# Small-head attention of a gated block stack: the order of scores, shifts, exponentials and additions on three engines

## The chip, the cores and the metric

The kernel runs on one core of a Trainium2 chip. The time is the device time of one execution in microseconds, and a lower one is better. The engines of the core are TensorE (PE; its weight loads are listed apart, as PEld), VectorE (DVE), ScalarE (ACT), GpSimd (POOL) and SyncE (SP, which here only issues DMAs). Each works off its own queue in the order written and waits on semaphores that the others raise.

## The reference, cut to what matters

The program takes `x` of 64 batch entries, each 128 rows of 128 values, and adds eight gated layers to it, four of them cross-attention to a context of 77 rows of 64 values for each batch entry. The change touches layer 0 and layer 2 of these, attention with 16 heads of 8 dimensions, which share one function:

```
x = x + tanh(g) * ATT(layernorm(x), ctx)
ATT: q = x @ Wq (+bq), k = ctx @ Wk (+bk), v = ctx @ Wv (+bv), each cut into 16 heads of 8
     scores = einsum('bhqd,bhkd->bhqk', q, k) / sqrt(8)
     out = einsum('bhqk,bhkd->bhqd', softmax(scores), v);  return concat(out) @ Wo (+bo)
```

All the other layers (expert feed-forward layers, two more attentions, a coupling network) stand unchanged.

## The kernel before, in words

`small_head_attention` (L535) is called twice, as stage `l0x` (L2947) and as stage `l2x` (L2951, with biases). A stage works through the 64 batch entries ("blocks" below, one block being one batch entry) in 16 rounds of `GROUP` = 4. What is done once for a round (the statistics and the normalizing of x, its transposes, queries, keys, two halves of the values) is spread over the four block slots of the round. Within a block the 16 heads are two halves, A and B, of eight heads, each half with a PSUM tile `scores[h]` of two banks.

The steps of one block, `j`, with the engine that takes each:

- `score` (TensorE, L751): six matmuls of half-precision parts write a half's scores.
- `max` (DVE, L965) reduces them to a maximum per head; `split_max` (GpSimd, L680 and L682) cuts it in two bf16 parts; `mt` (TensorE, `turn_max`, L758) transposes them; `m` (ScalarE, `fetch_max`, L882) brings them to `mT`; `shift` (TensorE, L767) adds minus the maximum to the scores in PSUM.
- `exp` (ScalarE, L889) writes the probabilities of the half to `probs`.
- The 1232 probabilities of a row are turned as ten pieces in three units: `turn0` (four pieces, needs only half A), `turn1` (four) and `turn2` (two), TensorE, L782. `high0` to `high2` (ScalarE, L895) and `rest0` to `rest2` (DVE, L969) make a high and a low half-precision part of each, and `weigh0` to `weigh2` (TensorE, L801, with filling matmuls L805) multiply by the values.
- `divide` (DVE, L977 and L981), `turn_o` (TensorE, L811), `o` (ScalarE, L901), `output` (TensorE, L815), and `add` (DVE, L989) into x.

`turned[0]` serves turn0 and turn2; `turned[1]` serves turn1, and holds the results of turn_o and output too, so turn1 waits until add of the block before has read it (`s_x`).

The order of the work is written by hand. Each engine has a text with the names of its steps in one slot; `slots` (L599) makes a list of it for the four slots of a round, and `skewed` (L43) runs this list for each round, with a lag for each step, so that steps of different rounds interleave. The last number of a step's entry, `ago`, tells of which block it is: 0 is the block `j` of the slot, 1 the block before it, 2 the one before that. In the kernel before, turn1, turn2, weigh0 to weigh2, divide, turn_o, output and add are of the block before, all else is of the block itself.

Work that belongs to the round goes in at `mid` and `end` of TensorE's text: the first slot has `q` at the end (queries, L716), the second `k` (keys, L721), the third `v0` (values of two blocks, L739), and the fourth `v1` (L739) at `mid` and `x` (transposes of the next normalized x, L362) at the end. The result of v0 and v1 is brought out by DVE (`block_values`, L957: v0 at `begin` of the fourth slot, v1 at its `mid`). All of q, k, v0, v1 and x write the same PSUM bank `pa`: `turn_x` waits on `s_vf` until block_values of v1 is done. On ScalarE, `x`, `q` and `k` are fetched at `begin` of the first three slots, and the parts of the values (L875, in two slots) or of the context (L845, in one) at `mid`.

Of the kernel before, what the change touches and what calls it, by code (L numbers as in the profile page):

```python
# [42 lines left out]
def skewed(eng, n, steps, lead):  # L43


    lead = min(lead, n)
    last = max(lag for _, lag in steps)
    assert lead % 2 == 0 and n % 2 == 0 and (n == lead or lead >= last + 2)

    def peeled(ts):  # L50
        for t in ts:
            for step, lag in steps:
                if 0 <= t - lag < n:
                    step(It(t - lag, (t - lag) // 2, (t - lag) % 2))

    peeled(range(lead))
    if n > lead:
        with eng.Fori(lead // 2, n // 2) as pair:
            for u in range(2):
                for step, lag in steps:  # L60
                    step(It(pair * 2 + (u - lag), pair + (u - lag) // 2, (u - lag) % 2))
    peeled(range(n, n + last))


def first_of(it):

    return isinstance(it.b, int) and it.b == 0
# [19 lines left out]
def nth(it, per=1, c=None, ago=0, back=0):  # L87


    value = it.b * per + ((per - 1 if c is None else c) + 1 - back - ago * per)  # L90
    return None if isinstance(value, int) and value <= 0 else value
# [110 lines left out]
class Softmax:  # L202
# [36 lines left out]
    def shift(self, dve, it, c):  # L239

        a, b = self.first[c], self.first[c + 1]
        dve.wait_ge(self.s_max, nth(it, self.nb, c))
        if (due := nth(it, self.nc_, ago=2)) is not None:
            dve.wait_ge(self.s_turn, due)
        dve.tensor_tensor(self.probs[it.par][:, a:b, :], self.view(c),  # L245
                          self.mx[it.par][:, a:b].unsqueeze(2).to_broadcast([P, b - a, self.keys]),
                          ALU.subtract).then_inc(self.s_shift, 1)

    def exponential(self, act, it, c):

        a, b = self.first[c], self.first[c + 1]
        act.wait_ge(self.s_shift, nth(it, self.nb, c))
        v = self.probs[it.par][:, a:b, :]
        act.activation(v, v, ACT.Exp, scale=self.scale).then_inc(self.s_exp, 1)  # L254
# [280 lines left out]
def small_head_attention(nc, g, name, wq, wk, wv, wo, bq=None, bk=None, bv=None, bo=None, gate=0):  # L535
# [14 lines left out]
    n = g.B // GROUP  # L550
    UNITS = [range(0, 4), range(4, 8), range(8, 10)]
    first_use = name == "l0x"
    with Stage(nc, name) as st:
# [37 lines left out]
        def half(h):  # L591

            return scores[h][:, :].rearrange("p (c f) -> p c f", f=BANK)[:, :, 0:W].rearrange("p c (h t) -> p c h t", t=KEYS)
# [5 lines left out]
        def slots(steps, order):  # L599


            out = []
            for j in range(GROUP):
                for step, lag, ago in [steps[k] for k in order[j].split()]:
                    out.append((lambda it, f=step, j=(j - ago) % GROUP: f(it, j), lag + (1 if j < ago else 0)))
            return out

        with nc.Block() as block:
# [94 lines left out]
            def _(pe):  # L703
# [5 lines left out]
                def turn_x(it):  # L709
                    if (due := nth(it, 2, ago=1)) is not None:  # L710
                        pe.wait_ge(s_vf, due)
                    fr.turn(pe, it)

                def queries(it):
                    pe.wait_ge(fr.s_xT, nth(it))
                    pe.matmul(pa[:, :], wq_s[:, :], fr.xT[it.par][:, :], start=True, stop=True).then_inc(s_q, 1)  # L716

                def keys_of(it):
                    pe.wait_ge(s_ctx[it.par], loads(it, 2))
                    pe.wait_ge(s_qlo, nth(it))  # L720
                    pe.matmul(pa[:, 0:GROUP * KEYS], wk_s[:, :], ctx2[it.par][0:CTX, :, :].rearrange("c b t -> c (b t)"),  # L721
                              start=True, stop=True).then_inc(s_k, 1)
# [32 lines left out]
                def turn_max(it, j, h):  # L755

                    pe.wait_ge(s_ml, nth(it, 8, 2 * j + h))
                    pe.matmul(scores[h][64 * h:64 * h + 64, W + 12:W + 12 + P], mh[j % 2][:, 2 * h:2 * h + 2, :].rearrange("p g r -> p (g r)"),  # L758
                              g.ident16[:, :], start=False, stop=True, skip_group_check=True).then_inc(s_mt, 1)

                def shift(it, j, h):
                    if first_of(it) and j == 0 and h == 0:
                        pe.wait_ge(g.s_made, CONSTANTS)
                    pe.wait_ge(s_mT, nth(it, 8, 2 * j + h))
                    for c in range(2):
                        rows = slice(64 * h + 32 * c, 64 * h + 32 * c + 32)
                        last = pe.matmul(scores[h][:, c * BANK:c * BANK + W], mT[j % 2][rows, :],  # L767
                                         g.minus_one[rows, :, :].rearrange("p h t -> p (h t)"), start=False, stop=True,
                                         skip_group_check=True)
                    last.then_inc(s_shift, 1)  # L770
# [42 lines left out]
                def output(it, j):  # L813
# [3 lines left out]
                steps = {"x": (lambda it, j: turn_x(it), 0, 0), "q": (lambda it, j: queries(it), 1, 0), "k": (lambda it, j: keys_of(it), 1, 0),  # L817
                         "v0": (lambda it, j: values(it, 0), 1, 0), "v1": (lambda it, j: values(it, 1), 1, 0),
                         "turn_o": (turn_o, 2, 1), "output": (output, 2, 1)}
                for h, half_name in enumerate("AB"):  # L820
                    steps["score" + half_name] = (lambda it, j, h=h: score(it, j, h), 2, 0)
                    steps["mt" + half_name] = (lambda it, j, h=h: turn_max(it, j, h), 2, 0)
                    steps["shift" + half_name] = (lambda it, j, h=h: shift(it, j, h), 2, 0)
                for u in range(3):
                    steps[f"turn{u}"] = (lambda it, j, u=u: turn(it, j, u), 2, 1 if u else 0)
                    steps[f"weigh{u}"] = (lambda it, j, u=u: weigh(it, j, u), 2, 1)
                fronts = [("", "q"), ("", "k"), ("", "v0"), ("v1", "x")]
                skewed(pe, n, slots(steps, ["scoreA turn1 turn2 weigh0 mtA weigh1 shiftA weigh2 scoreB turn0 " + mid +
                                            " turn_o mtB output shiftB " + end for mid, end in fronts]), 6)

            @block.scalar
            def _(act):
# [14 lines left out]
                def fetch_x(it):  # L847
                    fr.fetch(act, it, s_q)
# [35 lines left out]
                def exponential(it, j, h):  # L884
                    act.wait_ge(s_shift, nth(it, 8, 2 * j + h))
                    if (due := nth(it, 12, 3 * j + 2, back=6)) is not None:
                        act.wait_ge(s_turn, due)
                    dst = probs[j % 2][:, 2 * h * W:2 * (h + 1) * W].rearrange("p (c h t) -> p c h t", c=2, t=KEYS)
                    act.activation(dst, half(h), ACT.Exp, scale=scale).then_inc(s_exp, 1)  # L889
# [7 lines left out]
                def fetch_o(it, j):  # L897
                    act.wait_ge(s_oTp, nth(it, 4, j))
                    if (due := nth(it, 4, j, back=2)) is not None:
# [3 lines left out]
                steps = {"c": (lambda it, j: context_high(it), 0, 0), "x": (lambda it, j: fetch_x(it), 1, 0),  # L903
                         "q": (lambda it, j: fetch_q(it), 1, 0), "k": (lambda it, j: fetch_k(it), 1, 0),
                         "v0": (lambda it, j: fetch_v(it, 0), 2, 0), "v1": (lambda it, j: fetch_v(it, 1), 2, 0), "o": (fetch_o, 2, 1)}
                for h, half_name in enumerate("AB"):
                    steps["m" + half_name] = (lambda it, j, h=h: fetch_max(it, j, h), 2, 0)
                    steps["exp" + half_name] = (lambda it, j, h=h: exponential(it, j, h), 2, 0)
                for u in range(3):
                    steps[f"high{u}"] = (lambda it, j, u=u: high(it, j, u), 2, 1 if u else 0)  # L910
                fronts = [("x", "v0"), ("q", "v1"), ("k", ""), ("", "c")]
                skewed(act, n, slots(steps, [begin + " high1 high2 mA expA " + mid + " high0 o mB expB" for begin, mid in fronts]), 6)

            @block.vector
            def _(dve):
# [68 lines left out]
                def add(it, j):  # L984
                    x = g.x[:, bass.ts(it.b * GROUP + j, P)]
                    if biased:
# [4 lines left out]
                steps = {"stats": (lambda it, j: statistics(it), 0, 0), "norm": (lambda it, j: fr.normalize(dve, it), 0, 0),  # L991
                         "q": (lambda it, j: query_rest(it), 1, 0), "k": (lambda it, j: key_rest(it), 1, 0),
                         "v0": (lambda it, j: block_values(it, 0), 1, 0), "v1": (lambda it, j: block_values(it, 1), 1, 0),
                         "divide": (divide, 2, 1), "add": (add, 2, 1)}
                for h, half_name in enumerate("AB"):
                    steps["max" + half_name] = (lambda it, j, h=h: maximum(it, j, h), 2, 0)
                for u in range(3):
                    steps[f"rest{u}"] = (lambda it, j, u=u: rest(it, j, u), 2, 1 if u else 0)
                fronts = [("", "", "stats"), ("q", "", "norm"), ("k", "", ""), ("v0", "v1", "")]
                skewed(dve, n, slots(steps, ["maxA rest1 rest2 " + begin + " maxB divide rest0 " + mid + " add " + end  # L1000
                                             for begin, mid, end in fronts]), 6)


# [2020 lines left out]
```

## Time and profile before

| | us |
|---|---|
| median of 3 runs | 6024.17 (6015.81 to 6030.27) |
| the profiled execution | 6007.85 |
| its span | 6006.1 |
| PE busy | 5001.8 (83%) |
| PE weight loads busy | 3632.7 (60%) |
| DVE busy | 3931.2 (65%) |
| ACT busy | 2730.1 (45%) |
| POOL busy | 2168.7 (36%) |
| mean granted clock of TensorE | 0.905 |

The shares are means over the whole program. The two stages that the change touches take 604 and 593 us of the span. PE's busy time comes from instructions that overlap, so a busy PE can still be short of its peak. The granted clock is 1.00 at 2.4 GHz and 0.50 at 1.2 GHz.

### The profile page before, as it was taken

What the parts mean: (1) busy time and instruction counts of PE and PEld (TensorE: products, weight loads), DVE (VectorE), ACT (ScalarE), POOL (GpSimd) and SP (SyncE); (2) the same over time, 40 slices, a digit from 0 to 9 for tenths busy, and PEclk for the clock granted to TensorE, in tenths of its full rate; (3) what the DMA queues carried; (4) which work ended last, traced back from release to release, by engine and by line L of the source; (5) the groups of instructions that cost most, each with busy time, mean ns of one, the idle gap of its engine ahead of it and who ended that gap; (6) DMA issues with size and microseconds to landing.
All of it is one profiled execution on the core that took longest, in us unless ns stands there. A gap on an engine that the chain in (4) does not pass through costs nothing. (4 is left out here: it accounts for less than half of the span.)

```text
span 6006.1 us, 133430 instructions
## 1 busy us (share of the span) xinstructions
PE 5001.8 (83%) x41659; PEld 3632.7 (60%) x41659; DVE 3931.2 (65%) x9897; ACT 2730.1 (45%) x5454; POOL 2168.7 (36%) x3095
## 2 busy tenths in 40 slices
PE   7999898999962798069997998898898799998888
PEld 4555466888862465045555665776776577776544
DVE  4555685777766333245555776888887688887544
ACT  3444475555540233034444554555554355554344
POOL 4333100111117100644332334777775733333300
PEclk8888898999985899578888998999999899999988
DMA  1000500000011343100000000000000000000000
GB/s 37 6 4 2 242 0 14 5 5 5 5 49 43 114 136 116 47 13 6 4 3 12 1 0 9 0 0 0 0 0 5 7 2 2 2 2 6 1 11 18
DMA packets 108941, 140.24 MB, mean 23 GB/s; under 512 B 35832, under 2 KB 83256, under 8 KB 103996
## 3 DMA queue, kind: packets, MB, share of 16 engines
q1 hardware_dynamic: 100544, 120.88, 6.0%
q0 software_dynamic: 8192, 16.79, 1.0%
q8 instruction: 108, 1.77, 0.1%
q14 instruction: 97, 0.79, 0.0%
HBM read 47.44 MB, written 58.72 MB: 18 GB/s over the span
## 5 line engine op out<-in xcount | busy, mean ns | idle before, releaser
L2175 POOL TENSOR_TENSOR l3a_probs<-l3a_probs,l3a_later 128x512 f32<-128x512 f32 x256 | 320.6, 1281 | 4.9 <-DVE l3a_total L2363 4.9
L2161 POOL TENSOR_TENSOR l3a_keys<-l3a_kT,head 128x2048 f32<-128x2048 f32 x64 | 230.4, 3600 | 232.5 <-ACT l3a_kT L2288 232.5
L1590 POOL DMA_INDIRECT l1c_rows<-l_rows,l1f_slots x128 | 122.2, 955 | 456.7 <-PEq L1582 402.4
L2223 PE MATMUL l3a_scores<-l3a_keys,l3a_qT 128*128 128x512 f32 x512 | 256.5, 604 | 4.2 <-POOL l3a_keys L2161 4.2
L170 POOL TENSOR_TENSOR l1x_ve<-l1x_mv,eps 128x1 f32<-128x1 f32 x64 | 12.1, 190 | 660.6 <-DVE l1x_mv L162 660.6
L298 PE MATMUL l3a_po<-l3a_vals,l3a_probsT 128*128 128x32 f32 x2048 | 247.8, 269 | 0.1
L298 PEld LDWEIGHTS l3a_po<-l3a_vals,l3a_probsT 128*128 128x128 f32 x2048 | 246.8, 192 | 0.4 <-ACT l3a_probsT L279 0.4
L1661 POOL TENSOR_TENSOR l2f_hid<-l2f_prod,l2f_route 128x512 f32<-128x512 f32 x128 | 152.1, 1193 | 256.6 <-DVE l2f_prod L1808 253.3
L254 ACT ACTIVATE l3a_probs<-l3a_probs 128x512 f32<-128x512 f32 x256 | 161.7, 632 | 181.6 <-DVE l3a_probs L245 176.4
L965 DVE TENSOR_REDUCE l0x_mx<-l0x_scores 128x8 f32<-128x616 f32 x128 | 102.4, 800 | 192.0 <-PE l0x_scores L751 191.6
L965 DVE TENSOR_REDUCE l2x_mx<-l2x_scores 128x8 f32<-128x616 f32 x128 | 102.3, 800 | 178.7 <-PE l2x_scores L751 177.7
L1509 PE MATMUL l1e_h<-l1e_xhi,l1f_parts 128*128 128x512 f16 x640 | 204.8, 381 | 9.6 <-DVE l1e_gated L1567 8.1
L284 DVE SCALAR_TENSOR_TENSOR l1x_loT<-l1x_turned,l1x_hiT 77x512 f16<-77x512 f32 x256 | 168.7, 679 | 48.8 <-ACT l1x_hiT L277 48.7
L2161 POOL TENSOR_TENSOR l3c_keys<-l3c_kT,head 128x1232 f32<-128x1232 f32 x64 | 144.0, 2251 | 155.9 <-ACT l3c_kT L2288 155.9
L277 ACT ACTIVATE l3c_hiT<-l3c_turned 77x512 f16<-77x512 f32 x256 | 150.2, 587 | 106.7 <-PE l3c_po L298 104.1
L1102 ACT ACTIVATE l0f_relu<-l0f_h,l0f_route 128x512 f32<-128x512 f32 x256 | 157.8, 687 | 84.5 <-DVE l0f_route L1141 45.1
L2223 PE MATMUL l3c_scores<-l3c_keys,l3c_qT 128*128 128x308 f32 x512 | 191.2, 455 | 1.0 <-POOL l3c_keys L2161 1.0
L284 DVE SCALAR_TENSOR_TENSOR l3c_loT<-l3c_turned,l3c_hiT 77x512 f16<-77x512 f32 x256 | 173.8, 679 | 20.0 <-ACT l3c_hiT L277 19.9
L1567 DVE TENSOR_TENSOR l1e_gated<-l1e_h,l1e_silu 128x512 f32<-128x512 f32 x160 | 110.7, 692 | 115.1 <-ACT l1e_silu L1541 115.1
L279 ACT COPY l3a_probsT<-l3a_turned 128x512 f32<-128x512 f32 x256 | 150.3, 587 | 77.7 <-PE l3a_turned L266 77.2
L277 ACT ACTIVATE l1x_hiT<-l1x_turned 77x512 f16<-77x512 f32 x256 | 144.5, 589 | 86.1 <-PE l1x_po L298 77.0
L237 DVE TENSOR_REDUCE l3a_mx<-l3a_scores 128x4 f32<-128x512 f32 x256 | 169.8, 684 | 20.3 <-issue 16.1
(581 smaller groups left out, 17366.9 us busy)
## 6 DMA issues: line engine op xcount, KB each, us to landing
l_rows<-l0f_zeros SPq DMA_DIRECT2D x34, 1024.0 KB, 26.1
l1f_parts<-l1f_split SPq DMA_DIRECT2D x40, 512.0 KB, 3.6
l1e_x_in<-l_rows SPq DMA_DIRECT2D x40, 256.0 KB, 2.9
l1f_down<-l1f_w SPq DMA_DIRECT2D x40, 256.0 KB, 2.3
l_rows<-l1e_y_out SPq DMA_DIRECT2D x40, 256.0 KB, 2.7
l1f_w<-in_L_W SPq DMA_DIRECT2D x16, 256.0 KB, 3.3
out_x<-x_res SPq DMA_DIRECT2D x16, 256.0 KB, 2.0
x_res<-in_x SPq DMA_DIRECT2D x1, 3840.0 KB, 12.4
```

The costliest lines, as they stand in the source:

```text
L237: dve.tensor_reduce(self.mx[it.par][:, a:b], self.view(c), AX, ALU.max).then_inc(self.s_max, 1)
L254: act.activation(v, v, ACT.Exp, scale=self.scale).then_inc(self.s_exp, 1)
L277: act.activation(self.hiT[c % 2][:, :], src, ACT.Copy, scale=SPLIT_EXP).then_inc(self.s_fetch, 1)
L284: dve.scalar_tensor_tensor(self.loT[c % 2][:, :], self.ps_turn[c % 2][0:self.keys, :], SPLIT_EXP, self.hiT[c % 2][:, :], ALU.mult, ALU.sub ...
L298: last = pe.matmul(out_of(h), p[c % 2][:, cols], v, start=(i == 0), stop=(i == len(products) - 1))
L965: dve.tensor_reduce(mx[j % 2][:, 2 * h:2 * h + 2, :], half(h), AX, ALU.max).then_inc(s_max, 1)
L1102: act.activation(relu[e][:, :], ps_h[e][:, :], ACT.Relu, scale=rt.w[it.par][:, j, e:e + 1]).then_inc(s_relu, 1)
L1509: last = pe.matmul(bank[:, :], parts[p][:, w, f], x[p][:, :], start=(k == 0), stop=(k == 2))
L1661: pool.tensor_tensor(hid[k % 2][:, :].rearrange("p (e m) -> p e m", m=M), prod[k % 2][:, :].rearrange("p (e m) -> p e m", m=M), rt.w[it.pa ...
L2161: pool.tensor_tensor(keys[it.par][:, :, :, :], kT[it.par][:, :, :].unsqueeze(2).to_broadcast([P, J, G4, T]), g.head32[:, :].unsqueeze(1).u ...
L2175: pool.tensor_tensor(v, v, later[:, :].unsqueeze(1).to_broadcast([P, 4, T]), ALU.mult).then_inc(s_masked, 1)
L2223: pe.matmul(scores[c][:, 0:G4 * T], qT[it.par][:, c, :], keys[it.par][:, c, :, :].rearrange("p h t -> p (h t)"), start=True, stop=True).th ...
```

## The change

It moves steps within the hand-written orders and changes three of the `ago` numbers; no instruction is added or taken away.

- TensorE: scoreB now comes before shiftA, weigh1 and weigh2; shiftB is done one slot later (`ago` 1 for B), right behind scoreA of the next block; weigh0 comes before turn1 and turn2; turn0 stands behind the round's `mid` work, not ahead of it.
- ScalarE: expB is done one slot later, first of all; mA comes before high2; `mid` comes before expA.
- DVE: add is of two blocks before (`ago` 2) and opens the slot, behind the `end` work of the slot before rather than ahead of it; the `begin` work comes before rest1 and rest2.

```diff
@@ tensor
-                    steps["shift" + half_name] = (lambda it, j, h=h: shift(it, j, h), 2, 0)
+                    steps["shift" + half_name] = (lambda it, j, h=h: shift(it, j, h), 2, h)
...
                 fronts = [("", "q"), ("", "k"), ("", "v0"), ("v1", "x")]
-                skewed(pe, n, slots(steps, ["scoreA turn1 turn2 weigh0 mtA weigh1 shiftA weigh2 scoreB turn0 " + mid +
-                                            " turn_o mtB output shiftB " + end for mid, end in fronts]), 6)
+                skewed(pe, n, slots(steps, ["scoreA shiftB weigh0 turn1 turn2 mtA scoreB shiftA weigh1 weigh2 " + mid +
+                                            " turn0 turn_o mtB output " + end for mid, end in fronts]), 6)
@@ scalar
-                    steps["exp" + half_name] = (lambda it, j, h=h: exponential(it, j, h), 2, 0)
+                    steps["exp" + half_name] = (lambda it, j, h=h: exponential(it, j, h), 2, h)
...
                 fronts = [("x", "v0"), ("q", "v1"), ("k", ""), ("", "c")]
-                skewed(act, n, slots(steps, [begin + " high1 high2 mA expA " + mid + " high0 o mB expB" for begin, mid in fronts]), 6)
+                skewed(act, n, slots(steps, ["expB " + begin + " high1 mA high2 " + mid + " expA high0 o mB" for begin, mid in fronts]), 6)
@@ vector
-                         "divide": (divide, 2, 1), "add": (add, 2, 1)}
+                         "divide": (divide, 2, 1), "add": (add, 2, 2)}
...
                 fronts = [("", "", "stats"), ("q", "", "norm"), ("k", "", ""), ("v0", "v1", "")]
-                skewed(dve, n, slots(steps, ["maxA rest1 rest2 " + begin + " maxB divide rest0 " + mid + " add " + end
+                skewed(dve, n, slots(steps, ["add maxA " + begin + " rest1 rest2 maxB divide rest0 " + mid + " " + end
                                              for begin, mid, end in fronts]), 6)
```

## Rows read from the trace of the kernel before

**Rows 1.** busy time of each engine, granted clock (PEclk), by stretch; the two attention stages

```profile
41.00:645.00 604.00, 545.64 (x5708) 332.25 (x5707) 327.26 (x767) 280.59 (x602) 210.18 (x456) 0.84 0.02 4
...
2597.00:3190.00 593.00, 533.43 (x5694) 326.70 (x5693) 327.82 (x765) 284.28 (x602) 228.77 (x471) 0.86 0.02 4
```

**Rows 2.** the same view, two rounds of four blocks in stage l0x

```profile
229.71:264.51 34.80, 31.19 (x365) 19.70 (x365) 20.94 (x51) 17.73 (x38) 13.61 (x30) 0.95 0.03 6
...
302.06:341.85 39.79, 36.40 (x364) 21.63 (x365) 21.00 (x51) 17.73 (x38) 13.61 (x30) 0.79 0.02 4
```

**Rows 3.** instructions in time, TensorE: start us, length us, engine, line, output<-input, count, [idle before]

```profile
284.70 0.30 PE L751 MATMUL l0x_scores<-l0x_keys_hi,l0x_q_hi 32*128 32x308 f16 x2
...
285.20 0.88 PE L782 MATMUL l0x_turned<-ident,l0x_probs 128*128 128x128 f32 x6
285.91 0.17 PE L801 MATMUL l0x_po<-l0x_v_hi,l0x_p_hi 128*128 128x18 f16 x1
...
287.27 0.19 PE L801 MATMUL l0x_po<-l0x_v_hi,l0x_p_hi 128*128 128x27 f16 x1
...
288.30 0.30 PE L767 MATMUL l0x_scores<-minus_one,l0x_mT 32*128 32x308 bf16 x2
...
288.78 0.30 PE L751 MATMUL l0x_scores<-l0x_keys_hi,l0x_q_hi 32*128 32x308 f16 x2
...
289.38 0.66 PE L782 MATMUL l0x_turned<-ident,l0x_probs 128*128 128x128 f32 x4
290.73 0.33 PE L811 MATMUL l0x_turned<-ident,l0x_o 128*128 128x128 f32 x1 [0.69 <-DVE l0x_o L981]
290.99 0.24 PE L758 MATMUL l0x_scores<-ident,l0x_mh 128*64 128x128 bf16 x1
291.41 0.49 PE L815 MATMUL l0x_turned<-l0x_wo,l0x_oT 128*128 128x128 f32 x2 [0.18 <-ACT l0x_oT L901]
...
292.07 0.18 PE L739 MATMUL l0x_pa<-l0x_wv_a,l0x_ctxT 128*128 128x16 f16 x1
```

**Rows 4.** the same view, ScalarE, same block

```profile
285.89 0.87 ACT L895 ACTIVATE l0x_p_hi<-l0x_turned 128x512 f16<-128x512 f32 x2 [0.59 <-PE l0x_turned L782]
...
288.65 0.68 ACT L889 ACTIVATE l0x_probs<-l0x_scores 128x616 f32<-128x616 f32 x1 [1.18 <-PE l0x_scores L767]
290.08 0.60 ACT L895 ACTIVATE l0x_p_hi<-l0x_turned 128x512 f16<-128x512 f32 x1 [0.75 <-PE l0x_turned L782]
291.10 0.27 ACT L901 COPY l0x_oT<-l0x_turned 128x128 f32<-128x128 f32 x1 [0.42 <-PE l0x_turned L811]
291.38 0.26 ACT L882 CAST l0x_mT<-l0x_scores 64x128 bf16<-64x128 f32 x1
```

**Rows 5.** the same view, VectorE, same block

```profile
286.52 1.02 DVE L969 SCALAR_TENSOR_TENSOR l0x_p_lo<-l0x_turned,l0x_p_hi 128x512 f16<-128x512 f32 x2 [0.41 <-ACT l0x_p_hi L895]
...
289.39 0.80 DVE L965 TENSOR_REDUCE l0x_mx<-l0x_scores 128x8 f32<-128x616 f32 x1 [1.45 <-PE l0x_scores L751]
290.10 0.25 DVE L977 RECIPROCAL l0x_recip<-l0x_po 128x16 f32<-128x16 f32 x1
```

**Rows 6.** the same view, TensorE, the end of the fourth block

```profile
299.17 0.66 PE L782 MATMUL l0x_turned<-ident,l0x_probs 128*128 128x128 f32 x4
299.67 0.17 PE L739 MATMUL l0x_pa<-l0x_wv_a,l0x_ctxT 128*128 128x16 f16 x1
...
300.67 0.31 PE L811 MATMUL l0x_turned<-ident,l0x_o 128*128 128x128 f32 x1
...
302.06 0.63 PE L362 MATMUL l0x_pa<-ident,l0x_xn 128*128 128x128 f32 x4
```

**Rows 7.** the same view, VectorE, the fourth block

```profile
301.11 0.71 DVE L957 TENSOR_TENSOR l0x_v_f<-l0x_pa,piece_mask 128x240 f32<-128x240 f32 x2
```

**Rows 8.** busy time and granted clock of TensorE around a clock fall

```profile
307.00:309.50 2.50, 1.50 (x11) 1.00 0.00 0
...
310.40:313.60 3.20, 3.20 (x12) 0.50 0.00 0
```

## The prediction, made before the change was run

> **What bounds the kernel now.** Start with the stretches by stage: the two attention stages take 604 and 593 us, 1197 of the 6006 us span, and nothing else is touched, so all gain and loss lies there. TensorE is busy 90% of them, DVE 54%, ACT 47%, POOL 35 to 39% [rows 1]. TensorE bounds them, in two ways: by the short pauses in each block slot, and by its clock, granted at 0.84 and 0.86 of full. Two rounds of the same 365 matmuls (within one) take 34.80 us at a mean clock of 0.95 and 39.79 us at 0.79 [rows 2]. The time at half clock is twice the missing share: 2 x 0.05 x 34.80 = 3.5 us, and 2 x 0.21 x 39.79 = 16.7 us. So 13.2 us more at half clock cost 4.99 us: 0.38 us for each.
>
> Next the timeline of one slot at full clock, from scoreA at 284.70 [rows 3 to 5]. In offsets from scoreA: turn1 at 0.50, weigh0 1.21, weigh1 2.57, shiftA 3.60, scoreB 4.08, turn0 4.68, turn_o 6.03, mtB 6.29, output 6.71, then shiftB, and the next work at 7.37. The reader should see the pauses: before turn_o the row shows 0.69 us (for DVE's o), before output 0.18 (for ACT's oT) [rows 3]. Why turn_o is late: scoreB comes late, so maxB runs at 289.39 for 0.80, and divide is queued behind it [rows 5]. Behind such a place the clock falls: 307.0 to 309.5 has TensorE busy for 1.50 of 2.50 us at full clock, and from 310.4 on the clock is 0.50, with TensorE busy all the time [rows 8]. In the fourth slot of a round v1 covers just this pause: turn0 at 299.17, v1 at 299.67, turn_o at 300.67 and x at 302.06, with no pause noted at these [rows 6].
>
> **The change, part by part.** No instruction is added, so all rests on which wait ends last. I lay the new order out by hand with the lengths of the rows, from scoreA = 0 at full clock. The spacings between starts: score 0.50 (284.70 to 285.20), shift 0.24 (half of the 0.48 from shiftA to scoreB, which hold shift and the short weigh2; weigh2 the same), turn1 with turn2 0.71, weigh1 1.03, weigh0 1.02 (285.91 to mtA; it and weigh1 have four pieces each, so I take what 287.27 to 288.30 shows), turn0 0.50 [rows 3, 6]. A mt I take as 0.17 (an estimate, inside its length of 0.24).
>
> *A slot with no v1.* scoreA 0, shiftB 0.50, weigh0 0.74 to 1.76. ExpB starts 0.35 behind shiftB (288.30 to 288.65) and takes 0.68, ready at 1.53, so turn1 starts at 1.76 without a wait [rows 3, 4]. mtA at 2.47, scoreB at 2.64 to 3.14. maxA, at 0.70 to 1.50 (a max starts 0.6 to 0.7 behind its score, 288.78 to 289.39) and the two POOL operations (some 0.5) are done by then. high1 starts 0.69 behind turn1 (285.20 to 285.89), at 2.45, and ends at 3.05 (0.60 [rows 4]); mA is queued behind it, 0.26, so shiftA can't go before 3.39: a pause of 0.25. rest1 ends at 3.77 (the two rests take 1.02, rest1 0.69 of it), weigh1 starts at 3.83 and ends 4.86, weigh2 5.10, a pause of 0.2. ExpA (3.74 to 4.42, or to 4.93 behind a 0.59 `mid`) is ready for turn0 at 5.10. maxB now runs at 4.12 behind rest2, ends at 4.92, and is no longer in front of anything late: divide waits on weigh2's end (5.17), is done at 5.88, and turn_o starts at 5.93, a pause of 0.34 instead of 0.69. But then ACT is late: high0 starts 0.70 behind turn0, 5.80 to 6.40; o is behind it, 6.42 to 6.69 [rows 3, 4]; output goes at 6.74, a pause of 0.38 instead of 0.18. Output 0.42, next work at 7.16. So 7.16 against 7.37: **0.21 gained in each of three slots, 0.63 a round.** What stood behind output (shiftB, expB) is hidden by the next scoreA and weigh0; what that cover hides is 1.0 us. The bounds of this gain are 0 (the pauses only moved) and 0.5 (the 0.69 pause gone and output's kept at 0.18) a slot.
>
> *The fourth slot.* v1 now stands ahead of turn0. It takes 1.00 (299.67 to 300.67 [rows 6]): weigh2 ends 5.10, v1 to 6.10, turn0 at 6.10. turn_o and mtB follow without a wait, but high0 runs only at 6.80 to 7.40 and o to 7.69, so output goes at 7.74: a pause of 0.7 where v1 used to cover. Behind high0 on DVE is rest0 (to 8.12), behind that block_values of v1, 0.71 [rows 7], to some 8.8, and x on TensorE waits for exactly that. x goes at 8.83, a pause of 0.7 behind output's end at 8.16, and with its 0.6 the slot ends at 9.4. Before, from turn0 (offset 4.68, the distance in rows 3) to x took 302.06 - 299.17 = 2.89, so x was at 7.57 and the slot ended at 8.1 to 8.2. **1.3 us lost a round**; bounds 0.7 (x alone waits, the rest as before) and 1.6.
>
> *Moves at no cost.* add behind stats (1.25 us) or norm (1.1): add was already last in DVE's slot, and turn1, which needs it, is now at 1.76 instead of 0.50; if that cover went, up to 1 us in two slots. The begin work ahead of rest1 (0.47 to 0.71) lies in DVE's idle time between 1.50 and 3.05. The context copy (0.95) ahead of expA lies in the fourth slot, where v1 hides it. POOL's order is unchanged; in its fullest slot it is free about when maxB ends. SP issues two context loads a round, a round ahead, and is not moved.
>
> *Sum at full clock:* 1.3 - 0.63 = 0.67 us a round, in 2 x 16 rounds 21 us. About a third of the stages' time is at half clock (2 x 0.16 = 0.32 [rows 1]); there TensorE's parts take longer and cover most of these pauses: 21 x 0.68 = 14 us.
>
> *The clock.* By rows 2 a us at half clock costs 0.38. In three slots the longest pause falls from 0.69 to under 0.4, but the sum of the pauses changes little and they still lie close together; in the fourth slot, which had none of weight, two of 0.7 now follow each other closely. I expect to lose one place where the clock was safe and to weaken three where it fell; on balance 1 us more at half clock a round, 0.38 x 32 = 12 us. Bounds: from 7 us less (the three slots mostly stay up; the means of 0.84 become 0.94) to 5 us more (a fourth place of fall in most rounds), that is -85 to +61 us. I stay near zero, because the work per pause hardly changes.
>
> This is where the Trainium skill speaks against counting the clock at all. The trace shows a fall behind pauses of under 0.7 us each [rows 3, 8]; the page "TensorE: Matmul & The Clock Gate", section "HAM oscillation — how this bites in real kernels", ties the fall to long waits for a DMA in each tile, of which there are none here. By that page of the Trainium skill the clock term is 0 and the sum 14 to 21; by the rows it is the largest unknown.
>
> **Forecast:** 14 + 12 = 26 us slower than the profiled execution's 6007.85, that is 6034; the median of the runs shown is 16 higher, 6024.17, so 6050 us.
>
> **The rivals.**
> 1. *The clock comes back (faster).* Place: the three slots without v1, between scoreB and output. For it: the longest pause is nearly halved, and a round at 0.95 shows how much is to be had. Against: the sum of the pauses there hardly falls, and the fourth slot gets worse. Price: 4 us less at half clock a round, 0.38 x 4 x 32 = 49 gained against 14 lost: 5989. It decides from 1.2 us less a round on (0.44 / 0.38). The section "A second HAM failure mode: psum-queue depth-cycling" of the Trainium skill's page "TensorE: Matmul & The Clock Gate" tells of a clock that swings by short pauses between groups of matmuls; the falls behind the 0.69 us pauses agree with it, so the rival stays possible.
> 2. *The fourth slot is repaid.* The long slot lets DVE and ACT get ahead, and the next slots gain what it lost, or ACT is less late for output than I think: 0 to 0.1 us a round, no change, 6024 to 6028.
> 3. *A round loses its clock in the fourth slot and keeps the old falls.* 4 us more at half clock a round, 49 + 14: 6087. For it: the pauses of rows 3 still total as much. Against: TensorE at half clock has few pauses, so falls can't follow each other closely.
>
> **How the numbers follow.** The forecast's own case (6036 to 6072) 0.45, rival 1 0.23, rival 2 0.17, rival 3 0.15. A measurement of this kernel tells 0.2%, 12 us, from no change. Rival 1 gives faster 0.20 (a part of it ends within 12 us); same takes rival 2 and the edges, 0.20; slower 0.60. The range leaves out one in ten on each side: 5995 to 6095.
>
> **What would show it.** In the new profile: turn_o's wait for DVE shrinks, and output's wait for ACT's oT grows from 0.2 to 0.4 in three slots and to 0.7 in the fourth; x waits there for block_values (L957), some 0.7, where it waited for nothing; a slot with no clock fall takes 7.1 to 7.2 plus its round's work, the fourth 9.4. Wrong it would be if x waits for nothing (then v1 is not where I put it), if TensorE's clock in the two stages leaves 0.80 to 0.86, or if the other 4800 us move at all.

## The result: 3.1% faster where 0.4% slower was forecast

| | us |
|---|---|
| before, median | 6023.43 (6015.81 to 6030.27) |
| changed, median | 5839.89 (5836.92 to 5840.84) |
| ratio, 95% interval | 0.9693 [0.9681, 0.9705] |
| profiled execution | 6007.85 before, 5840.04 changed |

The forecast was 6050 in a range of 5995 to 6095: wrong in sign and outside the range.

Start again with the stretches. In each kernel I take a stage from its first query matmul to its last, 15 rounds: before first, then the changed kernel. Columns: stretch, its length, TensorE's busy time (instructions), granted clock, DMA share, GB/s.

```profile
30.30:578.30 548.00, 493.76 (x5207) 0.85 0.02 5
2585.60:3124.50 538.90, 483.12 (x5207) 0.85 0.02 5
```

```profile
30.40:500.30 469.90, 411.53 (x5206) 0.95 0.02 6
2490.30:2959.70 469.40, 408.90 (x5205) 0.94 0.02 6
```

The 15 rounds lose 78 and 70 us, 148 of the 168 us between the two spans. What lies between the stages (with the last rounds, which drain in it) goes from 2007.3 to 1990.0 us, and what follows from 2881.6 to 2878.3. So most of the change is where it was expected; its size was not.

The other 21 us are not simply a gain. No kernel here changes the instructions of those two parts, and still in the 13 traces of this case the part between takes 1975.2 to 2007.3 us and the part behind 2868.9 to 2892.1. Why is open. Where two kernels differ by 30 us or less, the lengths of the two stages tell more than the whole time, though each comes from one trace; the table below has both.

Look at the clock next. In stage l0x half-clock time falls from 2 x 0.15 x 548 = 164 us to 2 x 0.05 x 470 = 47 us, in l2x from 162 to 56. At the 0.38 us each that [rows 2] gave, that is, as an estimate, 44 and 40 us of the 78 and 70. The rest, 34 and 30 us, is a shorter round at full clock. A round of the changed kernel with no fall and one with a fall, as in [rows 2]:

```profile
167.42:198.90 31.48, 27.51 (x365) 17.87 (x365) 21.01 (x51) 16.63 (x38) 13.58 (x29) 1.00 0.03 7
231.16:264.56 33.40, 29.73 (x364) 19.09 (x365) 20.83 (x51) 16.77 (x38) 13.57 (x29) 0.90 0.02 5
```

Between these two a microsecond at half clock costs only 1.92 / 6.7 = 0.29 us; experiment e5 below gives 0.37 for the kernel before, close to the 0.38 used.

Now TensorE in the slot that answers to [rows 3], at full clock:

```profile
281.39 0.30 PE L751 MATMUL l0x_scores<-l0x_keys_hi,l0x_q_hi 32*128 32x308 f16 x2
281.41 0.30 PE L767 MATMUL l0x_scores<-minus_one,l0x_mT 32*128 32x308 bf16 x2
...
281.88 0.18 PE L801 MATMUL l0x_po<-l0x_v_hi,l0x_p_hi 128*128 128x18 f16 x1
...
282.82 0.82 PE L782 MATMUL l0x_turned<-ident,l0x_probs 128*128 128x128 f32 x6
283.58 0.24 PE L758 MATMUL l0x_scores<-ident,l0x_mh 128*64 128x128 bf16 x1
283.75 0.30 PE L751 MATMUL l0x_scores<-l0x_keys_hi,l0x_q_hi 32*128 32x308 f16 x2
...
284.26 0.30 PE L767 MATMUL l0x_scores<-minus_one,l0x_mT 32*128 32x308 bf16 x2
284.84 0.19 PE L801 MATMUL l0x_po<-l0x_v_hi,l0x_p_hi 128*128 128x27 f16 x1 [0.28 <-DVE l0x_p_lo L969]
...
285.93 0.63 PE L782 MATMUL l0x_turned<-ident,l0x_probs 128*128 128x128 f32 x4
286.75 0.33 PE L811 MATMUL l0x_turned<-ident,l0x_o 128*128 128x128 f32 x1 [0.19 <-DVE l0x_o L981]
287.01 0.24 PE L758 MATMUL l0x_scores<-ident,l0x_mh 128*64 128x128 bf16 x1
287.44 0.49 PE L815 MATMUL l0x_turned<-l0x_wo,l0x_oT 128*128 128x128 f32 x2 [0.18 <-ACT l0x_oT L901]
287.76 0.17 PE L739 MATMUL l0x_pa<-l0x_wv_a,l0x_ctxT 128*128 128x16 f16 x1
```

The slot took 7.37 us in [rows 3] and takes 287.76 - 281.39 = 6.37 here; I had laid it out at 7.16. The pauses noted are 0.28, 0.19 and 0.18 instead of 0.69 and 0.18. The first two lines are the surprise: scoreA and shiftB start 0.02 us apart, and weigh0 follows 0.49 behind scoreA. And ScalarE and DVE in the same slot, answering to [rows 4, 5]:

```profile
283.46 0.60 ACT L895 ACTIVATE l0x_p_hi<-l0x_turned 128x512 f16<-128x512 f32 x1 [0.44 <-PE l0x_turned L782]
283.96 0.25 ACT L882 CAST l0x_mT<-l0x_scores 64x128 bf16<-64x128 f32 x1
```

```profile
285.03 0.79 DVE L965 TENSOR_REDUCE l0x_mx<-l0x_scores 128x8 f32<-128x616 f32 x1
286.11 0.26 DVE L977 RECIPROCAL l0x_recip<-l0x_po 128x16 f32<-128x16 f32 x1 [0.29 <-PE l0x_po L801]
```

maxB now ends before divide can start: the reciprocal waits for TensorE's weigh2, not for maxB. The fourth slot, TensorE and then DVE, against [rows 6, 7]:

```profile
293.40 0.17 PE L739 MATMUL l0x_pa<-l0x_wv_a,l0x_ctxT 128*128 128x16 f16 x1
...
294.40 0.64 PE L782 MATMUL l0x_turned<-ident,l0x_probs 128*128 128x128 f32 x4
294.88 0.27 PE L811 MATMUL l0x_turned<-ident,l0x_o 128*128 128x128 f32 x1
...
295.88 0.49 PE L815 MATMUL l0x_turned<-l0x_wo,l0x_oT 128*128 128x128 f32 x2 [0.56 <-ACT l0x_oT L901]
297.27 0.63 PE L362 MATMUL l0x_pa<-ident,l0x_xn 128*128 128x128 f32 x4 [0.90 <-DVE l0x_v_f L957]
```

```profile
295.71 0.69 DVE L969 SCALAR_TENSOR_TENSOR l0x_p_lo<-l0x_turned,l0x_p_hi 128x512 f16<-128x512 f32 x1 [1.54 <-ACT l0x_p_hi L895]
296.31 0.71 DVE L957 TENSOR_TENSOR l0x_v_f<-l0x_pa,piece_mask 128x240 f32<-128x240 f32 x2
```

Here the forecast holds: output waits 0.56 for ScalarE (0.7 expected), x 0.90 for block_values (0.7 expected), and from scoreA at 288.85 to the next at 297.91 the slot takes 9.06 us, where I had 9.4. In the trace of before a fourth slot at full clock takes 8.13 (370.55 to 378.68).

### The profile page after: what moved, and what is told of

Same layout as the page of the kernel before. It is cut to its first block and busy times, and to the rows that moved or that the text cites. A ratio compares the mean times of both kernels' runs of the same rounds, so it can differ in the third digit from the quotient of the medians.

```text
span 5838.0 us, 133520 instructions
## 1 busy us (share of the span) xinstructions
PE 4832.9 (83%) x41659; PEld 3562.3 (61%) x41659; DVE 3930.2 (67%) x9897; ACT 2695.8 (46%) x5454; POOL 2168.9 (37%) x3095
## 5 line engine op out<-in xcount | busy, mean ns | idle before, releaser
L969 DVE SCALAR_TENSOR_TENSOR l0x_p_lo<-l0x_turned,l0x_p_hi 128x512 f16<-128x512 f32 (+1 forms) x192 | 110.1, 600 | 106.7 <-ACT l0x_p_hi L895 106.6
L254 ACT ACTIVATE l1x_probs<-l1x_probs 128x462 f32<-128x462 f32 (+1 forms) x192 | 97.8, 540 | 181.7 <-DVE l1x_probs L245 181.5
```

## The experiments

Each ran in three timed rounds beside the kernel before. Their ratios to it, with 95% intervals, the time of the two stages together (15 rounds each, as above, in the profiled execution) and the mean clock in them:

| run | median us | ratio to before | two stages, us | clock l0x, l2x |
|---|---|---|---|---|
| the kernel before | 6023.43 | 1 | 1086.9 | 0.85, 0.85 |
| the change itself | 5839.89 | 0.9693 [0.9681, 0.9705] | 939.3 | 0.95, 0.94 |
| e1 before, scoreB early | 5799.68 | 0.9632 [0.9607, 0.9656] | 898.2 | 0.97, 0.95 |
| e2 before, shiftB and expB later | 6148.67 | 1.0210 [1.0183, 1.0236] | 1227.9 | 0.75, 0.73 |
| e3 changed, scoreA and shiftB parted | 5919.60 | 0.9836 [0.9811, 0.9861] | 1019.6 | 0.91, 0.88 |
| e4 changed, same matmul beside | 5839.38 | 0.9702 [0.9677, 0.9727] | 942.0 | 0.95, 0.94 |
| e5 before, pause filled | 5963.49 | 0.9897 [0.9877, 0.9917] | 1045.9 | 0.92, 0.93 |
| e6 changed, turn0 ahead of v1 | 5793.36 | 0.9613 [0.9593, 0.9633] | 888.2 | 1.00, 0.97 |
| e7 changed, values ahead of rest0 | 5783.37 | 0.9600 [0.9581, 0.9619] | 886.2 | 1.00, 0.97 |
| e8 changed, both | 5781.72 | 0.9591 [0.9573, 0.9609] | 881.4 | 1.00, 0.97 |
| e9 changed, DVE's order of before | 5849.13 | 0.9721 [0.9704, 0.9737] | 963.3 | 0.95, 0.92 |
| e10 e8, round work at mid | 5738.13 | 0.9537 [0.9521, 0.9552] | 854.3 | 1.00, 0.97 |
| e11 before, same filling elsewhere | 6075.32 | 1.0098 [1.0081, 1.0115] | 1160.6 | 0.88, 0.86 |

**e1: one step of the change alone.**

```diff
-scoreA turn1 turn2 weigh0 mtA weigh1 shiftA weigh2 scoreB turn0
+scoreA turn1 turn2 weigh0 mtA scoreB shiftA weigh1 weigh2 turn0
```

> The kernel before with one step moved: scoreB ahead of shiftA, weigh1 and weigh2; shiftB, expB and add stay where they were. Theory 1 (the late maxB kept divide and turn_o waiting, and taking that pause out is what gives the time and the clock): a slot at full clock falls from 7.37 to about 6.8 us, the clock of the two stages rises from 0.85 to over 0.92, 5850 to 5910 us. Rival (the gain of the change comes from shiftB beside the next scoreA and expB a slot later): here only a small part of it, 5970 to 6030 us, clock 0.84 to 0.88.

Better than theory 1 said: 5799.68. Moving scoreB alone gives more than the whole change. TensorE in a slot at full clock with the keys at its end (265.07 to 272.49, of which 0.72 is the keys), 6.70 us to the keys:

```profile
267.61 0.30 PE L751 MATMUL l0x_scores<-l0x_keys_hi,l0x_q_hi 32*128 32x308 f16 x2
...
268.34 0.19 PE L801 MATMUL l0x_po<-l0x_v_hi,l0x_p_hi 128*128 128x27 f16 x1
...
270.36 0.33 PE L811 MATMUL l0x_turned<-ident,l0x_o 128*128 128x128 f32 x1 [0.29 <-DVE l0x_o L981]
...
271.12 0.49 PE L815 MATMUL l0x_turned<-l0x_wo,l0x_oT 128*128 128x128 f32 x2 [0.26 <-ACT l0x_oT L901]
```

turn_o's pause is 0.29 instead of 0.69, and no weigh1 waits, because weigh0 still lies between turn1 and it.

Like must be compared with like. The slot of the changed kernel that ends with keys takes 6.73 to them, against 6.70 here. The slot of e1 that ends with v0, as the one of [rows 3] does, runs from 242.61 to 248.91, and its turn_o waits 0.18:

```profile
242.61 0.30 PE L751 MATMUL l0x_scores<-l0x_keys_hi,l0x_q_hi 32*128 32x308 f16 x2
...
247.57 0.33 PE L811 MATMUL l0x_turned<-ident,l0x_o 128*128 128x128 f32 x1 [0.18 <-DVE l0x_o L981]
...
248.91 0.18 PE L739 MATMUL l0x_pa<-l0x_wv_a,l0x_ctxT 128*128 128x16 f16 x1
```

That is 6.30 us, where before had 7.37 and the change 6.37. So in these slots all of the gain comes with the moved scoreB, and the rest of the change adds none. Of the 1.07 us, 0.53 lie between turn0 and turn_o (1.35 before, 0.82 here), where the pause was. Another 0.53 lie between mtA and turn0 (2.45 before, 1.92 here), in weigh1, weigh2, scoreB and shiftA; no run parts these into their causes.

**e2: the other part alone.**

```diff
-scoreA turn1 turn2 weigh0 mtA weigh1 shiftA weigh2 scoreB turn0 (mid) turn_o mtB output shiftB
+scoreA shiftB weigh0 turn1 turn2 mtA weigh1 shiftA weigh2 scoreB turn0 (mid) turn_o mtB output
-ScalarE: (begin) high1 high2 mA expA (mid) high0 o mB expB
+ScalarE: expB (begin) high1 high2 mA expA (mid) high0 o mB
```

> The kernel before with the other part alone: shiftB and expB one slot later, weigh0 ahead of turn1 as in the change, but scoreB still behind shiftA, weigh1 and weigh2. Theory 1: weigh1 now follows turn1 closely and waits for high1 and rest1 (2.05 us behind turn1), a new pause of about 1 us in each slot, turn_o's wait stays; 6060 to 6150 us, clock 0.75 to 0.84. Rival (scoreA and shiftB side by side and a shorter end of the slot are worth it by themselves): 5930 to 6000 us.

```profile
288.66 0.89 PE L782 MATMUL l0x_turned<-ident,l0x_probs 128*128 128x128 f32 x6
...
290.83 0.19 PE L801 MATMUL l0x_po<-l0x_v_hi,l0x_p_hi 128*128 128x27 f16 x1 [1.10 <-DVE l0x_p_lo L969]
...
294.38 0.33 PE L811 MATMUL l0x_turned<-ident,l0x_o 128*128 128x128 f32 x1 [0.62 <-DVE l0x_o L981]
```

Theory 1's, both pauses where it put them; the clock of l2x, 0.73, is just below its range. The later shiftB needs the earlier scoreB, which fills the place between turn1 and weigh1; without it this part costs 2.1%.

**e3 and e4: are scoreA and shiftB side by side?** One matmul of 8 columns over all rows of the array (`apart`), between them or behind them.

```diff
-scoreA shiftB weigh0
+scoreA apart shiftB weigh0        (e3)
+scoreA shiftB apart weigh0        (e4)
```

> The changed kernel with one matmul of 8 columns over all 128 rows put between scoreA and shiftB. Theory 1 (these two work on different rows of the array, 0 to 63 and 64 to 127, and run at the same time, which saved the 0.24 us that I had summed for shiftB): the two no longer overlap, 0.2 to 0.35 us more a slot against a kernel with the same matmul beside them, in 128 slots 25 to 45 us. Rival (shiftB is cheap for another reason): no more than 5 us against that kernel.

> The changed kernel with the same matmul of 8 columns behind shiftB, where it parts nothing: the price of the matmul itself, 0 to 0.1 us a slot, 5840 to 5853 us by both theories.

TensorE in e3:

```profile
254.53 0.30 PE L751 MATMUL l0x_scores<-l0x_keys_hi,l0x_q_hi 32*128 32x308 f16 x2
...
255.03 0.18 PE L810 MATMUL l0x_po<-l0x_blank 128*128 128x8 f16 x1
255.14 0.30 PE L767 MATMUL l0x_scores<-minus_one,l0x_mT 32*128 32x308 bf16 x2
255.38 0.18 PE L801 MATMUL l0x_po<-l0x_v_hi,l0x_p_hi 128*128 128x18 f16 x1
```

From scoreA to weigh0 it is 0.85 us, against 0.49 in the changed kernel and 0.54 in e4 (248.41 to 248.95). In the whole time the matmul itself costs nothing that can be measured (e4). Parting the two costs 80 us against e4, more than the 25 to 45 expected. The two stages grow by 77.6 us. The slot with v0 goes from 7.48 in e4 to 7.81, and 0.33 in each of 120 slots is 40 us. Two pauses in l2x, of 3.50 and 4.97 us and a shorter one behind each, in which TensorE waits for nothing that the profile shows, are 10.8 us more; e4 has none. The rest, some 27, goes with the mean clock, which falls by 0.04 and 0.06; its size was not foreseen. The overlap is shown, by the starts 0.02 us apart and by the 0.24 us that shiftB takes again once it is parted (255.14 to 255.38). That it is worth something against another order is not: e1, without it, has the shorter slot.

**e5 and e11: is it the clock?** Five matmuls of zeros (256 columns), in three slots of a round, in the kernel before.

```diff
-... turn0 turn_o mtB ...
+... turn0 fill turn_o mtB ...     (e5)
-... weigh2 scoreB turn0 ...
+... weigh2 fill scoreB turn0 ...  (e11)
```

> The kernel before, its order unchanged, with five matmuls of zeros (256 columns each, some 0.55 us at full clock) ahead of turn_o in the three slots that have no v1, where TensorE stood 0.69 us; their result is read by nobody. Theory 1 (the larger part of the gain is the clock, which fell behind this pause): the clock of the two stages rises from 0.85 to 0.93 or more and the time falls by 60 to 130 us, to 5890 to 5960, though no wait is any shorter. Rival (the pauses cost by their own length, the clock follows something else): 6020 to 6050 us, clock 0.84 to 0.87.

> The kernel before with the same five matmuls of zeros in three slots as in e5, but ahead of scoreB, where TensorE has no pause, so that they lengthen the slot and leave turn_o's pause of 0.69 us as it is. Theory 1 (the clock follows the pauses): clock 0.84 to 0.87 as before, 0.55 us more in 96 slots, 6060 to 6100 us. Rival (the clock follows how much TensorE streams, wherever it is put): clock 0.89 to 0.93, which pays for the longer slot, 5990 to 6040 us.

The two stages in e5, then in e11:

```profile
30.20:561.30 531.10, 483.15 (x5417) 0.92 0.02 6
2562.60:3077.40 514.80, 466.80 (x5417) 0.93 0.03 6
```

```profile
30.10:609.40 579.30, 506.51 (x5417) 0.88 0.02 6
2601.50:3182.80 581.30, 508.71 (x5417) 0.86 0.02 6
```

In e11 turn_o still waits:

```profile
290.73 0.33 PE L817 MATMUL l0x_turned<-ident,l0x_o 128*128 128x128 f32 x1 [0.80 <-DVE l0x_o L987]
```

With nothing made earlier, only the pause filled, the kernel gets 1.03% faster and the stages run at 0.92 and 0.93, a little short of what theory 1 said. The same filling ahead of the pause makes it 0.98% slower, the clock 0.03 and 0.01 above before.

Both times hold something that the filling brought with it. TensorE stands still for 3.1 to 3.7 us before scoreA at the start of a round, eight times in e5 and eight in e11, and waits for nothing that the profile shows; never in the kernel before. The first in e5:

```profile
245.80 0.44 PE L751 MATMUL l0x_scores<-l0x_keys_hi,l0x_q_hi 32*128 32x308 f16 x2 [3.40 <-issue]
```

With the shorter ones behind them, such pauses are 30 us in each of the two kernels, and the clock falls behind them too (0.80 from 245.80 to 285.51 in e5). Their cause is open. They weigh on e5 and e11 alike, so the 112 us between the two stand. What filling does by itself shows in the first five rounds of l0x, taken from the first scoreA on; both kernels have none of these pauses there:

| five rounds of l0x | us | mean clock |
|---|---|---|
| before, 41.66 to 230.27 | 188.61 | 0.85 |
| e5, 41.49 to 208.86 | 167.37 | 1.00 |
| e11, 41.41 to 229.12 | 187.71 | 0.92 |

With the pause filled the clock does not fall at all, and the 57 us at half clock that are gone give back 21.2, 0.37 for each. With the same matmuls elsewhere and the pause left, about half of the loss of clock goes as well, which pays for the longer slots. So filling this one pause is enough to end the falls of before. That nothing but the pause matters is not shown: e11's 0.92 is what its rival expected, and it leaves room for how much TensorE does elsewhere in the slot.

**e6, e7, e8: the fourth slot.**

```diff
-TensorE: ... weigh2 (mid) turn0 turn_o ...      +TensorE: ... weigh2 turn0 (mid) turn_o ...   (e6, e8)
-DVE: ... maxB divide rest0 (mid) ...            +DVE: ... maxB divide (mid) rest0 ...         (e7, e8)
```

> The changed kernel with turn0 ahead of the round's mid work on TensorE again, so v1 stands between turn0 and turn_o. Theory 1 (the fourth slot lost some 1 us a round since high0, rest0 and block_values all wait behind v1): x's pause of 0.9 us falls below 0.3 and output's of 0.56 goes; 0.7 to 1.2 us a round, 5800 to 5820 us. Rival (the fourth slot's length is set elsewhere): 5835 to 5845 us.

> The changed kernel with block_values of v1 ahead of rest0 on DVE in the fourth slot, where DVE stands idle 1.5 us waiting for high0. Theory 1: x's pause of 0.9 us goes, output's of 0.56 stays: 0.6 to 0.9 us a round and the clock fall of the fourth slot, 5800 to 5820 us. Rival: something else holds x, 5835 to 5845 us.

> The changed kernel with both: turn0 ahead of v1 on TensorE, and block_values of v1 ahead of rest0 on DVE. Theory 1: as good as the better of the two by up to 10 us, 5795 to 5815 us; block_values now waits for v1's end and rest0 behind it, which nobody needs before the next weigh0. Rival: rest0 is now late for weigh0, 5820 to 5840 us.

All three are 0.8 to 1.1% better than the change (46 to 58 us; 51 to 58 in the two stages), somewhat more than expected, with the clock of l0x at 1.00. The falls of the changed kernel lay mostly in the first slot of a round, behind the fourth, and either correction ends them. What is left in l2x, 0.97, lies at its start. The fourth slot of l0x at full clock takes 7.8 us in e8 in most rounds, 7.9 in e7 and 8.0 to 8.1 in e6, against 9.0 in the change. e8 is not told from e7. Against e1 it is better by 0.4%, with intervals that just meet: its rounds at full clock are no shorter (30.2 us against 30.0), but they keep the clock.

**e9: DVE's part undone.**

```diff
-add maxA (begin) rest1 rest2 maxB divide rest0 (mid) (end)      add of two blocks before
+maxA rest1 rest2 (begin) maxB divide rest0 (mid) add (end)      add of the block before
```

> The changed kernel with DVE's order of before: add of the block before and ahead of stats or norm, and the round's begin work behind rest1 and rest2, so between them and maxB. Theory 1 (the forecast's: DVE's part of the change is worth nothing by itself): 5830 to 5850 us. Rival (with scoreB early, maxB is what divide and turn_o wait behind, and 0.47 to 0.71 us of begin work ahead of it delays turn_o in three slots a round): 5855 to 5910 us, clock below 0.94 in the two stages.

The median, 5849.13, is at the upper edge of theory 1, and by the ratios (0.9721 against 0.9693, intervals that just touch) DVE's part is worth 0 to 0.5%. The stages say more. They take 963.3 us against 939.3, 24 us longer, while the parts that nobody touched happen to be 23 us shorter in this trace (4845.6 against 4868.3). And the wait is the rival's: turn_o waits up to 0.54 us for DVE in l0x (at 247.80) and 0.60 in l2x, against 0.29 in the change, and the second slot of a round in l0x takes 7.85 instead of 7.44. So by the stages DVE's part is worth some 24 us. That is from one trace of each kernel; e4, whose time is that of the change, is 2.7 us away from it by the same measure.

**e10: round work at mid.**

```diff
-fronts = [("", "q"), ("", "k"), ("", "v0"), ("v1", "x")]
+fronts = [("q", ""), ("k", ""), ("v0", ""), ("v1", "x")]
```

> The kernel with both corrections of the fourth slot (e8), and the queries, the keys and the first half of the values put between turn0 and turn_o as well, as v1 is, not at the end of the slot. Theory 1 (these round works cover what is left of turn_o's wait for DVE, 0.2 to 0.3 us in three slots): 0.15 to 0.3 us a slot, 5755 to 5772 us against 5782. Rival (ScalarE's o behind high0 holds output anyway and the slot keeps its length): 5778 to 5786 us.

```profile
30.30:456.20 425.90, 390.35 (x5201) 1.00 0.02 6
2431.40:2859.80 428.40, 390.61 (x5201) 0.97 0.02 6
```

The best kernel here: 4.6% below before, 1.7% below the change. The time fell by more than expected, but not by this change alone: the stages take 854.3 us against 881.4, 27 us less and the upper end of theory 1, and the other 22 between the two profiles lie in the parts that nobody touched. turn_o waits for DVE in none of the 15 rounds of either stage, as theory 1 said.

## Why the prediction was wrong, by its own steps

- **"So 7.16 against 7.37: 0.21 gained in each of three slots".** This term failed: 7.37 to 6.37, 1.00 gained, twice the upper bound of 0.5. The laid-out order reads 0.79 too long, in these places. A quarter of a microsecond was shiftB, summed as 0.24 of its own; it runs beside scoreA, on other rows of the array (e3, e4). The trace of before could not show it, since there these two were never neighbours, but the Trainium skill states it: the page "TensorE: Matmul & The Clock Gate", section "Why this matters for your kernels", says that small matmuls in distinct row groups run at the same time. The row agrees: starts 0.02 us apart. Five spacings were read too long, by 0.68 together: weigh0 0.94 for 1.02, weigh1 with weigh2 1.09 for 1.27, turn1 to shiftA 1.44 for 1.63, turn0 to output 1.51 for 1.64, output to next 0.32 for 0.42. One was read too short, shiftA to weigh1, 0.58 for 0.44. In two of the five ScalarE's operations were laid end to end, where the trace has the next start some 0.1 before the end of the one before (mA at 283.96, o at 287.12). For the other three the spacings of the old order did not hold in the new one, and no run says why. The forecast also never asked what one moved step gives alone: e1 shows that scoreB by itself gives this whole term, and that what shiftB saves beside scoreA comes back as weigh1's wait of 0.28.
- **"1.3 us lost a round" in the fourth slot.** Right in place and mechanism; before, the slot took 8.13, now 9.06, so 0.9 lost, inside the bounds of 0.7 to 1.6. e6 to e8 confirm it, and against e8's 7.8 it is 1.2. That the slot's length came out near 9.4 is partly luck: v1 started at 4.55, where 5.10 was laid out, and x 0.25 behind the end of block_values, where 0.03 was.
- **"1 us more at half clock a round".** This step failed in sign. Half-clock time a round went from 10.9 us to 3.1 in l0x and from 10.8 to 3.8 in l2x: 7.0 to 7.8 us less, at and over the bound of 7 I gave. I argued that the sum of the pauses hardly changes. They changed: in the slot the noted pauses went from 0.87 to 0.65, in a shorter slot with the longest only 0.28, and the clock fell no longer in the second and third slot, but behind the fourth. e5 shows that filling the one pause of 0.69 is enough: 0.92 and 0.93 in the stages, and 1.00 over five rounds.
- **The rivals.** Rival 1, the clock coming back, was the true one, at 1.7 times its price (84 us, the estimate above for the 30 rounds, for 49), beside a gain of order it had not: it was given 0.23. Rivals 2 and 3 are out.
- **The first section cited from the Trainium skill** ("HAM oscillation — how this bites in real kernels", long waits) would have had no clock term. The rows and e5 speak against it here: no single pause before was over 0.7 us in the slots shown, and the clock is the larger half of what the stages gained, 84 of 148 us. The section "A second HAM failure mode: psum-queue depth-cycling" of the same page of the Trainium skill tells of short idle times between groups of matmuls behind which the clock swings; the rows and e5 agree with it.
- **"Moves at no cost"** held for the cost, but DVE's part was put at nothing where it gains: by the stages of e9 some 24 us of the 148, with begin in DVE's idle time ahead of rest1, and not between rest2 and maxB. e9 undoes this and add's move together and does not part them.
- **"if the other 4800 us move at all".** They moved by 21 us, of which the last rounds of a stage are a few. By its own sign this speaks against the forecast; but they move as much between kernels that differ elsewhere, so the sign was a poor one.
- **What bounds the kernel** held: maxB ahead of divide was the wait to remove, and e1, which moves only scoreB, gives 3.7%. The wait is half of what e1 gains in a slot at full clock; the other half came unforeseen.

## What to carry to other kernels

Where TensorE's clock falls behind a recurring short pause, price the pause by the clock too: here filling one of 0.69 us, in three slots of four, gave 1% though nothing got earlier, and moving one step, which took most of it away and half a microsecond besides, gave 3.7%. Try the steps of a reordering one by one: here one alone did better than all of them. Spacings read between instructions belong to the order that they were read in; laid end to end in a new order they overstated it (0.8 us in a slot of 6.4 here), and two matmul steps on disjoint rows that became neighbours took the time of the longer. After such a reordering look at the one slot of a round that differs: of the 85 us that e10 still took from the two stages of the changed kernel, 58 lay there. And read a small difference in the stage that was changed: the rest of this program moves by up to 30 us from kernel to kernel.

## What the hardware showed that was not expected

- scoreA (rows 0 to 63) and shiftB (rows 64 to 127) take 0.49 us together; with a matmul of 8 columns over all rows between them 0.85, and with the same matmul behind both 0.54.
- Five matmuls of zeros in a pause bring the clock of the two stages from 0.85 to 0.92 and 0.93 and the time down by 1.03%; placed ahead of scoreB they cost 0.98%. Over the first five rounds the clock is 1.00 with the pause filled, 0.92 with the filling elsewhere, 0.85 without any.
- Three of the four kernels with added matmuls (e3, e5, e11) have rare pauses of 3 to 5 us on TensorE before scoreA, in which it waits for nothing that the profile shows; e4, with as many added as e3, has none. The cause is open.
- ScalarE starts mA at 283.96 though high1, started at 283.46 for 0.60 us, ends at 284.06.
